# GNN message loop on one Trainium2 core: the two instructions that split a group's edge attributes on VectorE are put into different steps

## What is computed

```python
src, dst = (edge_index[0], edge_index[1])
edge_feat = jnp.concatenate([x[src], x[dst], edge_attr], axis=-1)   # 512 + 512 + 64
h = mish(edge_feat @ W1 + b1)
messages = mish(h @ W2 + b2)
agg = jax.ops.segment_sum(messages, dst, num_segments=x.shape[0])
u = mish(jnp.concatenate([x, agg], axis=-1) @ W3 + b3)
out = u @ W4 + b4
...                                                                  # x + out, layer norm
```

## Time and profile before

| | |
|---|---|
| median of 3 runs | 1686.47 us (1679.83 to 1688.41) |
| the profiled execution, its own time | 1686.17 us |
| its span in the profile | 1684.5 us |
| the message loop in that span | about 940 to 1630 us |
| PE busy | 1574.1 us, 93% |
| DVE busy | 1207.3 us, 72% |
| ACT busy | 1083.4 us, 64% |
| POOL busy | 687.0 us, 41% |

### The profile page before, as it was taken

One profiled execution on the slowest core, in us unless ns is written; L12 is line 12 of the kernel. 1 busy time (PEld: TensorE's weight loads), 2 busy tenths in 40 slices (PEclk: granted clock), 3 DMA queues, 4 the chain that ended last, 5 costly groups with the idle time before them and its releaser, 6 DMA issues. The chain is left out here.

```text
span 1684.5 us, 25118 instructions
## 1 busy us (share of the span) xinstructions
PE 1574.1 (93%) x8530; PEld 1222.6 (73%) x8530; DVE 1207.3 (72%) x1923; ACT 1083.4 (64%) x1494; POOL 687.0 (41%) x495
## 2 busy tenths in 40 slices
PE   4889599999999999999999999999999999999987
PEld 4765396788687868877854777777777777777874
DVE  8987536564656556564733489898989899898977
ACT  8851326553654555444510599999999999999962
POOL 3520200011012001200302688888888888888600
PEclk9999699999999999999999999999999999999989
DMA  3001420004002201111007777777777777777710
GB/s 103 0 0 39 125 84 29 1 32 131 26 7 69 88 25 32 57 56 47 19 1 251 151 150 140 152 145 147 144 148 144 145 147 136 156 139 152 165 38 31
DMA packets 107047, 153.94 MB, mean 91 GB/s; under 512 B 42043, under 2 KB 47035, under 8 KB 106467
## 3 DMA queue, kind: packets, MB, share of 16 engines
q0 software_dynamic: 72832, 87.84, 27.3%
q1 hardware_dynamic: 34146, 65.21, 12.0%
HBM read 141.02 MB, written 11.73 MB: 91 GB/s over the span
## 5 line engine op out<-in xcount | busy, mean ns | idle before, releaser
L1626 POOL DMA_INDIRECT edge_gathered<-dst_table,edge_index x158 | 257.0, 1627 | 57.6 <-issue 54.3
L222 PE MATMUL edge_z2p<-edge_w_hi,edge_h_hi 128*128 128x512 f32 x628 | 255.2, 406 | 6.1 <-DVE edge_late L1927 4.7
L1595 POOL DMA_INDIRECT edge_gathered<-src_table,edge_index x158 | 221.6, 1403 | 94.9 <-issue 32.7
L222 PE MATMUL edge_z2p<-edge_w_hi,edge_h_lo 128*128 128x512 f32 x628 | 248.5, 396 | 0.0
L222 PE MATMUL edge_z2p<-edge_w_lo,edge_h_hi 128*128 128x512 f32 x628 | 248.3, 395 | 0.0
L880 POOL TENSOR_TENSOR tr_r<-tr_r,tr_row_b 128x512 f32<-128x512 f32 x40 | 59.2, 1516 | 277.2 <-ACT C L1115 277.0
L869 POOL TENSOR_TENSOR tr_cw<-tr_cw_raw,tr_cw 32x1024 fp32r<-32x1024 f32 x8 | 19.0, 2369 | 358.3 <-ACT tr_cw L1076 358.3
L222 PEld LDWEIGHTS edge_z2p<-edge_w_hi,edge_h_hi 128*128 128x128 f32 x628 | 117.9, 188 | 60.5 <-issue 35.6
L1944 DVE SCALAR_TENSOR_TENSOR edge_early<-edge_early,edge_z1p 128x1024 f32<-128x1024 f32 x79 | 96.5, 1221 | 59.7 <-ACT edge_early L1826 59.7
L222 PEld LDWEIGHTS edge_z2p<-edge_w_hi,edge_h_lo 128*128 128x128 f32 x628 | 118.0, 188 | 28.5
L222 PEld LDWEIGHTS edge_z2p<-edge_w_lo,edge_h_hi 128*128 128x128 f32 x628 | 118.1, 188 | 25.0
(11 more groups left out here) (338 smaller groups left out, 4012.6 us busy)
## 6 DMA issues: line engine op xcount, KB each, us to landing
edge_attr<-in_attr_T SPq DMA_DIRECT2D x78, 128.0 KB, 5.4
tr_w_raw<-in_m SPq DMA_DIRECT2D x8, 1024.0 KB, 5.4
agg<-edge_sum_rows POOLq DMA_DIRECT2D x36, 128.0 KB, 10.5
tr_w_raw<-in_wv SPq DMA_DIRECT2D x4, 1024.0 KB, 5.4
tr_w_raw<-in_wq SPq DMA_DIRECT2D x4, 1024.0 KB, 5.4
tr_w_raw<-in_wk SPq DMA_DIRECT2D x4, 1024.0 KB, 6.7
tr_w_raw<-in_wo SPq DMA_DIRECT2D x4, 1024.0 KB, 6.7
tr_cw_raw<-in_cond_w SPq DMA_DIRECT2D x4, 768.0 KB, 5.8
```

The source lines that it names most:

```text
L222: mm = pe.matmul(out, a, b, start=(n == 0), stop=(n == last))
L1595: pool.indirect_dma_start(out=from_rows[a][:, j, :].bitcast(F32), out_offset=None, in_=k.src_table, in_offset=bass.IndirectOffsetOnAxis(ap ...
L1626: pool.indirect_dma_start(out=from_rows[ring][:, j, :].bitcast(F32), out_offset=None, in_=k.dst_table, in_offset=bass.IndirectOffsetOnAxis ...
```

## The change

The cast is taken out of the even step and put at the end of the odd step ahead of it, for the group of the even step that follows. The subtraction stays where it was, at the end of the even step. The very first group has both in step 0. The wait for `z1_made` moves with the cast and counts one more, because the cast stands one step earlier: the slot's last reader on PE is in step a-1 then.

```diff
+                def attr_high(slot, group):
+                    dve.wait_ge(attr_loaded[slot], group // 2 * 32 + 32)
+                    dve.tensor_copy(attr_parts[slot][:, :], attr[slot][:, :]).then_inc(S["attr_high"], 1)
...
                     if a % 2 == 0 and on(0):
 
                         slot = a // 2
-                        dve.wait_ge(attr_loaded[slot], g(0) // 2 * 32 + 32)
-                        if on(4):
-
-                            dve.wait_ge(S["z1_made"], s(-2))
-                        dve.tensor_copy(attr_parts[slot][:, :], attr[slot][:, :]).then_inc(S["attr_high"], 1)
+                        if not on(1):
+                            attr_high(slot, g(0))
                         dve.wait_ge(S["attr_high"], g(-2))
                         dve.tensor_tensor(attr_parts[slot][high, :], attr[slot][high, :], attr_parts[slot][high, :].bitcast(F32),
                                           ALU.subtract).then_inc(S["attr_low"], 1)
+                    if a % 2 == 1 and on(-1):
+
+                        if on(3):
+
+                            dve.wait_ge(S["z1_made"], s(-1))
+                        attr_high((a + 1) % 4 // 2, g(-1))
```

## The result

Over 20 executions each, the median went from 1684.01 us (1679.11 to 1688.41) to **1679.80 us** (1677.38 to 1682.89). The ratio is 0.9979, with a 95% interval from 0.9969 to 0.9988: a gain of 0.21%, about 3.5 us, surely there and under the 0.5% that was called no change. The time forecast was 1679.5; the saving forecast was 7.0 us. The profiled execution of after took 1678.64 us, 7.5 less than the 1686.17 of before. So the forecast sum fits the two traces, and not the two medians; much of what follows is on that gap.

The account below looks back on a forecast made before the run. The ACT and DVE chain, 17.14 us in two steps, was taken as the bound, with PE second at 16.94. Savings of 6.5 in the loop and 0.5 at the start made 7.0, giving 1679.5 us; range 1675.5 to 1689.0.

Parts of the forecast that it names:

- The size in the loop: Message loop: PE's lost 0.20 us in each of 32 pairs of steps is saved, 6.5 us.
- The start: First steps of the message loop: PE loses 1.1 us there; saving between 0 and 1.1, taken as 0.5 us.
- The long half: Longer distance between ACT's L1822 starts: without the cast it goes from 9.18 to 8.63 us, or 8.44 if POOL doesn't disturb.
- near 8.5 and 8.4: Sign in the loop after the change: L1822's two distances in us, instead of 7.96 and 9.18.
- How close L1966 may follow: DVE, even step: L1966 starts 1.26 us after L1955 starts, held until it finishes; long half 8.63, without the rule 8.51.
- The short half: Shorter distance between L1822 starts, with the moved cast on DVE: 7.94 to 8.30 us, taken as 8.16; ACT's queue 7.96.
- some disturbance is likely: Moved cast, beside POOL's index copy and gathers: POOL stretches it, not more than at the old place; short half 8.16 us.
- Rival 1: POOL becomes the loop's bound as its gather ends later: slower from a 17.36 us round, examples 1689.4 and 1696; chance 0.13.
- Rival 2: Cast and both L1901 held up 0.14 to 0.25 us more: chain 17.0 to 17.2, time 1682 to 1687; chance 0.13.
- Rival 3: The cast's place doesn't matter for L1901, as ACT's L1816 comes as late: no difference, 1686 us; chance 0.05.
- Rival 4: More than PE's 0.20: slow start and end shrink by 1.5 us too, 1677 us or less; chance 0.07.
- it lies 0.3 under the median, so the median would be 1679.5: Last step of the sum: the profiled execution of 1686.17 becomes 1679.2, and 0.3 is added for the median.

Follow-up runs that it names:

- lighter after: The changed kernel with 8 of PE's 16 attribute matmuls of a step left out: 1668.82 us, ratio 0.9886 against before.
- lighter pair: The kernel before and the changed kernel, each with 8 of PE's 16 attribute matmuls of a step left out: 1686.63 and 1668.82 us.
- b_shift3: The kernel before with two memsets of a spare tile on POOL, once, ahead of step 15: 1686.38 us, ratio 1.0017; profiled execution 1680.09 us.
- second trace of before: The kernel before, unchanged, profiled once more: 1685.63 us; the 14 executions beside it have a median of 1686.31 us.

## Why the prediction was right, and where it was not

- **What bounds the loop before** (chain of ACT and DVE, PE second by 0.20): right for the executions that were traced. A lighter PE leaves it at 17.154 in two steps.
- **PE becomes the bound at 16.94**: right, 16.947 in two steps throughout; a lighter PE then pays at once.
- **The size in the loop**, 6.5 us: 6.45 in the traces. **The start**, 0.5 taken: the gap narrows by 1.0 up to the 13th turn (1035.12 against 1034.10), of which 0.36 is there before the first turn (939.59 against 939.23) and not the change's. **The end**, 0: from the 77th turn to the end of the span it is 100.6 in both.
- **The long half**, 8.44 to 8.63, and the sum 16.79: near in the lighter after (8.63 and 16.75), in part by luck: L1966 followed by L1904 took 0.72 and not 0.78, and L1904 0.88 and not 0.83. Undisturbed, the sum was 16.40 (the casts at 990.19 to 1023.00). In after itself the distances are 8.99 and 7.96, not the "near 8.5 and 8.4" that the prediction gave as a sign. That sign was thought out wrongly: with PE as the bound, DVE's L1931 waits for PE's product in the long half and carries ACT with it, so L1822 shows how PE's 16.95 is split, not the length of its own chain. For the same reason ACT waits for L1905 in one half and not in both.
- **How close L1966 may follow**: 1.26 was taken, and 1.25 measured (1199.23 to 1200.48), where the cast follows the same kind of instruction after 1.14 (1207.69 to 1208.83). By the rule of the Trainium skill ("VectorE: DVE Perf Modes", section "Two Vector instructions with no wait between them") the first is held until the instruction ahead has finished, since its inputs start in another quadrant, and the second is not. The trace agrees; the hold is worth 0.11 us here.
- **The short half**: 8.16 was taken, with a cast stretched by 0.22. In after the cast came at 0.42 in all 32 groups of the 64 steps, in the lighter after at 0.42 to 0.47, and the half there at 8.05. The step "some disturbance is likely" was wrong for after, on the safe side: the cast falls into POOL's gap behind the index copy.
- **Rival 1**, POOL as the bound: fell. It keeps PE's pace, and its gather behind the copy got shorter by 1.0, not longer. **Rival 2**, more disturbance: fell, there is less. **Rival 3**: fell by the lighter pair. **Rival 4**: the start gave 1.0, of which 0.7 is the change's, and not the 1.5 or more that it needed.

**The step that failed** is the last of the sum: "it lies 0.3 under the median, so the median would be 1679.5". The number came out (1679.80), but the saving didn't: 4.2 between the medians and 3.5 by the ratio, not 7.0. The base of three executions, 1686.47, was 2.5 above the median of twenty, 1684.01, because executions of before differ. That the time came out so well is thus in part luck: the same 7.0 taken from 1684.01 would have given 1677.0. Of its twenty, 6 are at 1679.1 to 1680.4 us, 5 at 1683.0 to 1684.3, and 9 at 1685.7 to 1688.4; the middle of the first six is 1679.8, the median of after, and that of the last nine 1687.1, which is 7.3 above it. All five traces of before that were taken (1685.6 to 1689.5 us) show a stretched cast and 17.12 to 17.15 in two steps; undisturbed runs of the old order (before pushed once, before without the store) show 16.947, at 1680.1 us in the first and 1683.8 in the second, so the five in the middle may be of either kind. If a third of before's executions are of that kind, the change has nothing to save in them, and 7 us in two thirds is 4.7, near what was measured. That reading rests on the b_shift3 trace with its two memsets and on the distribution; a short execution of the unchanged kernel before was not caught in a trace, so it is likely, not shown. Beside the second trace of before only 1 of 14 executions of before lay under 1684, beside before pushed once 6 of 12, so the share itself differs from one set of executions to the next. The prediction named this ("if such a run is one in which POOL didn't disturb DVE") and used it for the width, not for the size; it should have been in the sum.

The range 1675.5 to 1689.0 holds the time; it was wide because of a rival with POOL that the chip didn't show at all.

## What to carry to other kernels

Where two chains of a software pipeline are nearly as long as the busiest engine's work, a change is worth the distance to that engine and not a bit more, and making that engine lighter, in a kernel of its own, shows at once which of the two bounds. Where a profiled distance contains operations that are longer than the same ones elsewhere in the trace, the gain exists only in executions in which they are: take the base from many executions and look at how they are spread before subtracting. A step that is taken off a chain by spreading it over two stages bought steadiness here too: after's twenty executions span 5.5 us, those of before 9.3.

## What the runs showed of the hardware

The same program falls into different, lasting patterns between VectorE and GpSimd's DMA issue. Three were seen in the old order: cast, subtraction and L1901 at 0.64, 0.75 and 0.83 us, with the cast starting 1.66 to 1.68 us behind the start of the store; at 0.77 to 0.80, 0.69 and 0.70 to 0.75, with the cast 0.3 us behind it; and all undisturbed, at 0.42 to 0.44, 0.69 and 0.69, with the cast 5.1 to 6.9 us behind it. In two of the five traces of before the first held through the loop; in three it passed into the second at about 1085 to 1100 us, which then stayed nearly to the end. Against the undisturbed one they cost 0.18 to 0.20 us in two steps, 6 us in all, and with an additional cast on VectorE the one execution traced was in an undisturbed pattern, so that the cast did not add its own length to a stretched round.

The stretching itself is partial. A cast of 0.42 us got 0.2 to 0.4 longer, beside a store issue of 2.05 us on GpSimd. The Trainium skill ("SBUF — State Buffer", section "Who interferes with whom") says that the later of the two fully blocks until the other instruction is through. By that the cast would have been held for the rest of the store: 0.4 us in the first pattern and 1.7 in the second (the cast at 1204.83, in a store from 1204.51 for 2.05). Measured are 0.22 and 0.35 to 0.38, so for these two kinds of work the measurement decides against the rule's full length. What after's lighter executions did, three at 1668.75 to 1671.18 and one at 1661.11 us, is open as well: the first kind was traced, the last not.
